# Two attention layers in one trunk: the value products move behind the next block's scores, and the second layer's V is made of nine products instead of twelve

## The chip, the cores and the metric

The kernel runs on one core of a Trainium2 chip, as one launch. The metric is the device time of a run in microseconds (us), as the median of three runs. Engines are named as the profile names them: PE (TensorE matmul; PEld is its weight load), DVE (VectorE), ACT (ScalarE), POOL (GpSimd), SP (the queue that issues most DMAs).

## The reference

The input is x, 16 sequences of 128 tokens with 128 features, and a context of the same shape. Four layers follow one another, each added to x:

```python
x = x + L0_xattn(ctx, layernorm(x), ctx)     # 16 heads of 64, causal mask, softmax over 128 keys
x = x + L0_ffn(layernorm(x))                 # FP4-quantised gate/up/down, 352 hidden
x = x + L1_xattn(layernorm(x), ctx)          # 16 heads of 64, two softmaxes:
#   keys 0..76  ("text"):  k = ctx @ Wk,    v = ctx @ Wv
#   keys 77..127 ("image"): k = ctx @ Wk_ip, v = ctx @ Wv_ip
#   out = (softmax_text @ v_text + softmax_image @ v_image) @ Wo + bo
x = x + L1_ffn(layernorm(x))                 # router, top 2 of 8 experts, 512 hidden
```

What matters for the change is the second attention layer's V: 77 keys of a sequence are multiplied by Wv and the other 51 by Wv_ip. The order of the keys is free, as long as the probabilities of a key meet the V row of the same key.

## The kernel before

The 16 sequences form 8 groups of two (PAIR); the 16 heads form 4 blocks of four (BLOCKS, HB). Both attention layers run in one trunk of 128 steps, n = 0 to 127: layer 0 is n 0 to 63, layer 1 is n 64 to 127. A group takes 8 steps, a block two: an even step and the odd step behind it, called a pair here. Each engine has its own function `step`, called for each n in turn (trunk, L366), so the order of the work on an engine is written out by hand, and each engine runs its list strictly in that order, held only by semaphores.

PE (step, L792), even step: the scores of the block, 16 matmuls (L815, each with 64 rows of the array); Q and K of the next block, three passes each (L404 to L406: low times high, high times low, high times high); the transposes of the probabilities of step n-2 (L853, 4 matmuls); the values, probabilities times V, of the block two pairs back (L868, 16 matmuls, each with 64 columns of the array). Odd step: V of the block (project_v, L646), the transposes (L853), the output projection with Wo (L885, 8 matmuls). V takes 6 matmuls in layer 0. In layer 1 the staged context is held twice, once with the text keys and zeros elsewhere (st_hi[0], st_lo[0]) and once with the image keys and zeros elsewhere ([1]), and V is the sum over both: 2 sequences x 2 weights x 3 passes = 12 matmuls.

ACT (L1037), even step: it copies Q and K from PSUM (L909, L916 or L924), the transposed probabilities (L1034) and the heads (L1027), and takes the exponential of the scores (L1068 in layer 0, L1072 in layer 1). Two switches (heads_first, probs_first) set the order of these copies. Odd step: it copies V (L1061), takes the exponential, then does the FFN's work of the step, then copies the transposed probabilities.

DVE (L1384): in an even step first the sums (L1361) of the odd step before, the update of x (L1111), the mask and maxima (L1333, L1339) or the maxima and the subtraction (L1351, L1377) of both steps of the pair, and the inverse of the sums (L1369). In layer 0 most sums of odd steps come from ACT's own accumulator instead. In an odd step: the sums and inverse of the even step.

POOL (L1614) scales the exponentials to probabilities (L1625, in layer 1 one instruction for the text keys and one for the image keys) and stages the context of the next group at the end of a group (stage, L1590).

The first FFN is woven in from n = 16 (ffn_at): its eight slots s0 to s7 fall on steps 0, 2, 3, 4, 5, 7, 8, 9 of each ten. Slot s0 has the back half of one quantisation on DVE, s1 its end, s2 the transposes and copies of the hidden layer (L658, L970), s3 the down product (L676) and the quantisation of x, s4 the gate product, a tanh on ACT (L979) and its product on DVE (L1307), s5 a transpose, s6 the up product, s7 a quantisation. The norm of x after layer 1 is woven in by D_AT: the four steps of each group of sequences at which its slots 4 to 7 run. In the last of them PE transposes into the bank of the probabilities (turn_d, L704), ACT copies the high part (L940) and DVE the low part (L1209). The transposes of the next step wait for that low part. From n = 114 the router of the experts is woven in (routes).

## Time and profile before

| | us |
|---|---|
| median of 3 runs (lowest, highest) | 666.07 (665.52, 667.85) |
| profiled execution, own time | 668.6 |
| its span | 666.9 |
| PE busy / PEld busy | 612.9 / 560.3 |
| DVE busy / ACT busy / POOL busy | 492.2 / 464.8 / 308.2 |
| mean granted TensorE clock | 0.969 |

A matmul's busy time is modelled and overlaps the next one's: a matmul of 0.28 us can be followed by another 0.12 us later. So the pace of PE is read from the distance between starts, and a "busy" PE can still hold short gaps. In the timeline a pair begins at the first matmul of L815.

### The profile page before, as it was taken

To read this page: it belongs to the slowest core of one execution; us is meant where nothing else is said; L and a number is where in the kernel's file an instruction comes from. 1 tells how busy PE (TensorE), PEld (TensorE's weight loads), DVE (VectorE), ACT (ScalarE), POOL (GpSimd) and SP (SyncE) were. 2 spreads that over 40 slices of the span, in tenths; PEclk is the share of its full clock that TensorE was granted. 3 is DMA by queue.
4 is the path that set the end of the run, shared out by engine and by line. 5 is a ranking of instruction groups with operands and counts; after the bars stand their busy time and mean duration, and the time that the engine had idled before them with its cause. 6 is when DMAs were issued, how large, how long until landed. Compare 5 with 4: busy or idle time off the path is not lost.

```text
span 666.9 us, 16387 instructions
## 1 busy us (share of the span) xinstructions
PE 612.9 (92%) x5665; PEld 560.3 (84%) x5665; DVE 492.2 (74%) x1255; ACT 464.8 (70%) x1347; POOL 308.2 (46%) x444
## 2 busy tenths in 40 slices
PE   5898999999999999999999999999999879989990
PEld 5787888988889899999989988888888868979990
DVE  6588787798887978888797986876655665656654
ACT  5987889988888896666666766667555354646762
POOL 4365344444444434354445343445265574456450
PEclk9998999999999999999999999999889798989995
DMA  9800000000000000336664020000000032112215
GB/s 221 260 2 1 1 1 1 2 2 2 1 2 2 2 17 2 128 79 125 124 123 93 25 57 1 1 2 2 1 21 25 21 103 57 49 57 65 70 51 198
DMA packets 49626, 33.33 MB, mean 50 GB/s; under 512 B 9524, under 2 KB 46104, under 8 KB 49544
## 3 DMA queue, kind: packets, MB, share of 16 engines
q1 hardware_dynamic: 47272, 27.61, 17.3%
q0 software_dynamic: 2272, 4.67, 2.1%
q8 instruction: 46, 0.75, 0.5%
q14 instruction: 36, 0.29, 0.2%
HBM read 17.64 MB, written 14.63 MB: 48 GB/s over the span
## 4 chain that ended last, share of the span: by engine, by line
PE 53%; issue 14%; DVE 11%; POOL 9%; ACT 8%; DMA 2%; SPq 0%; POOLq 0%; DVEq 0%; another core or an unknown queue 0%; ACTq 0%
PE ps_j L646 6%; PE ps_h L868 6%; PE ps_s L815 6%; PE ps_h L885 5%; PE ps_t L853 5%; PE ps_j L404 4%; ACT scores L1068 4%; PE ph L1811 4%; PE py L1822 3%; POOL probs L1625 3%; POOL xs_scratch L1736 3%; PE ps_j L405 3%; PE ps_j L406 3%; PE pf L676 2%; DVE sums L1361 1%
## 5 line engine op out<-in xcount | busy, mean ns | idle before, releaser
L1625 POOL TENSOR_TENSOR probs<-scores,rsums 128x308 f32<-128x308 f32 (+1 forms) x192 | 152.2, 807 | 202.4 <-DVE rsums L1369 202.1
L1068 ACT ACTIVATE scores<-scores,neg_max 128x128 f32<-128x128 f32 x256 | 91.7, 398 | 0.0
L1034 ACT ACTIVATE probsT<-ps_t 128x512 f32<-128x512 f32 x128 | 76.4, 597 | 18.5 <-PE ps_t L853 18.2
L853 PE MATMUL ps_t<-ident,probs 128*128 128x128 f32 x512 | 79.4, 278 | 5.5 <-POOL probs L1625 4.4
L1361 DVE TENSOR_REDUCE sums<-scores 128x4 f32<-128x308 f32 (+2 forms) x156 | 66.3, 459 | 23.2 <-ACT scores L1072 11.7
L909 ACT ACTIVATE QT<-ps_j 128x512 f32<-128x512 f32 x64 | 38.3, 598 | 51.9 <-PE ps_j L406 51.9
L868 PE MATMUL ps_h<-probsT,V 128*64 128x128 f32 x1024 | 71.1, 281 | 2.3 <-DVE x_sb L1111 2.3
L885 PE MATMUL ps_h<-Wo,headsT 128*128 128x128 f32 x512 | 69.8, 280 | 2.0 <-ACT headsT L1027 1.9
L853 PEld LDWEIGHTS ps_t<-ident,probs 128*128 128x128 f32 x512 | 60.4, 143 | 9.4 <-POOL probs L1625 7.3
L885 PEld LDWEIGHTS ps_h<-Wo,headsT 128*128 128x128 f32 x512 | 63.8, 196 | 3.4 <-ACT headsT L1027 3.4
L868 PEld LDWEIGHTS ps_h<-probsT,V 128*64 128x64 f32 x1024 | 55.6, 138 | 13.2 <-issue 11.7
L646 PE MATMUL ps_j<-l_hi,st_lo 128*128 128x256 f32 x192 | 61.2, 319 | 0.9 <-ACT QT L909 0.9
L815 PE MATMUL ps_s<-KT,QT 64*128 64x128 f32 x800 | 59.0, 288 | 0.8 <-ACT KT L916 0.8
L1872 ACT ACTIVATE hT<-ph,w1s 128x128 f32<-128x128 f32 x156 | 45.5, 371 | 16.4 <-PE ph L1811 13.9
L1891 POOL DMA_INDIRECT y_scratch<-ysb,xt x39 | 38.6, 991 | 37.6 <-DVE ysb L1948 35.0
L646 PE MATMUL ps_j<-l_hi,st_hi 128*128 128x256 f32 x192 | 55.6, 290 | 0.0
L646 PE MATMUL ps_j<-l_lo,st_hi 128*128 128x256 f32 x192 | 55.6, 289 | 0.0
L815 PEld LDWEIGHTS ps_s<-KT,QT 64*128 64x128 f32 x800 | 49.4, 190 | 7.0 <-issue 1.9
L1351 DVE TENSOR_REDUCE neg_max<-ps_s 128x8 f32<-128x616 f32 x64 | 42.4, 663 | 16.5 <-PE ps_s L815 16.5
L1061 ACT ACTIVATE V<-ps_j 128x512 f32<-128x512 f32 x64 | 37.8, 590 | 23.0 <-PE ps_j L646 22.9
L1027 ACT ACTIVATE headsT<-ps_h 128x512 f32<-128x512 f32 x64 | 38.3, 598 | 20.1 <-PE ps_h L868 20.0
L1811 PE MATMUL ph<-xT,w1s 128*128 128x128 f32 x312 | 44.3, 284 | 5.0 <-ACT hT L1872 3.2
(248 smaller groups left out, 1640.2 us busy)
## 6 DMA issues: line engine op xcount, KB each, us to landing
xs_scratch<-xs SPq DMA_DIRECT2D x8, 1032.0 KB, 8.3
xt<-xs_scratch SPq DMA_DIRECT2D x39, 64.5 KB
w1b<-in_L_ffn_w_dram SPq DMA_DIRECT2D x1, 2048.0 KB, 10.4
big_raw<-in_L_ffn_w_dram SPq DMA_DIRECT2D x8, 256.0 KB
ysum<-y_scratch SPq DMA_DIRECT2D x4, 512.0 KB, 5.3
Wo<-in_L_xattn_Wo_dram SPq DMA_DIRECT2D x2, 512.0 KB, 5.2
out_dram<-x_sb SPq DMA_DIRECT2D x4, 256.0 KB, 2.4
x_sb<-in_x_dram SPq DMA_DIRECT2D x3, 256.0 KB, 9.2
```

Source lines behind the costliest of these rows:

```text
L646: ins = nc.tensor.matmul(dst, st[i][:, bb, :], w[:, cols], start=(n == 0), stop=(n == 3 * len(SEGS[lay]) - 1))
L815: ins = nc.tensor.matmul(ps_scores[half][:, j * S:(j + 1) * S], QT[hb % 2][rows, t, bb, :], k_home(m)[rows, t, bb, :], start=True, stop=True)
L853: ins = nc.tensor.transpose(ps_pT[:, j * S:(j + 1) * S], probs[s % 2][:, j, :], ident[:, :])
L868: ins = nc.tensor.matmul(ps_heads[par * HD:(par + 1) * HD, (bb * TILES + t) * S:(bb * TILES + t + 1) * S], V[hr % 2][:, bb, i * HD:(i + 1) ...
L885: ins = nc.tensor.matmul(ps_heads[:, bb * D:(bb + 1) * D], headsT[:, bb, t, :], Wo[lr][:, hr * TILES + t, :], start=(t == 0), stop=(t == T ...
L1034: nc.scalar.activation(probsT[(s - 2) % 4][:, :, :].rearrange("p h s -> p (h s)"), ps_pT[:, :], ACT.Copy).then_inc(SS["pT_copied"], 1)
L1068: ins = nc.scalar.activation(scores[s % 4][:, j, :], scores[s % 4][:, j, :], ACT.Exp, bias=neg_max[:, 0, s % 4, j:j + 1], **total)
L1351: nc.vector.tensor_reduce(pair_of(neg_max[:, i, :, :], s).rearrange("p t h -> p (t h)"), pair_bank()[:, :, k0:k1], AX_X, ALU.max, negate=T ...
L1361: ins = nc.vector.tensor_reduce(sums[:, p4, i, :], scores[p4][:, :, k0:k1], AX_X, ALU.add)
L1625: ins = nc.gpsimd.tensor_tensor(probs[(s - 1) % 2][:, :, k0:k1], scores[r][:, :, k0:k1], rsums[:, r, i, :].rearrange("p (h a) -> p h a", a ...
L1811: ins = nc.tensor.matmul(ph[k // 2][:, (k % 2) * P:(k % 2 + 1) * P], w1s[i % 3][:, 0, k * P:(k + 1) * P], xT[i % 2][:, :], start=True, sto ...
L1872: nc.scalar.activation(hT[i % 2][:, k, :], ph[k // 2][:, (k % 2) * P:(k % 2 + 1) * P], ACT.Silu, bias=w1s[i % 3][:, 0, HID + k:HID + k + 1 ...
```

## The change

Two things are changed. (1) On PE the values go to the front of the even step, directly behind the scores, and the output projection goes to the end of the same even step; before, the values ended the even step and the output ended the odd one. ACT copies the heads first in an even step; it copies the transposed probabilities before it takes the exponential, in odd steps before it copies V too. DVE updates x in the odd step, behind both steps' maxima. The router's middle part goes ahead in odd steps, and D_AT is changed so that the last slot of a norm falls on an even step. (2) In layer 1 the staged context gets a new layout of 128 key columns: one copy holds text keys only, 64 of sequence 1 and 64 of sequence 0 (st[0], column 0); one holds the 13 text keys left over of each (st[1], column 0); one holds the 51 image keys of both (st[0], column 1). The first makes one half of the bank in three passes with Wv, the other two make the other half in three passes with Wv and three with Wv_ip: 9 matmuls. The keys of a sequence so stand in a rotated order, and the upper 64 rows of the two halves are swapped. V is copied by three ACT instructions (64 partitions x 512, and twice 64 x 256), POOL writes the probabilities with three instructions, and the staging of a group takes 12 casts for 4.

```diff
+        HALF, IP = S // 2, S - TEXT
+        MIXED = TEXT - HALF
...
-        D_AT = [(81, 83, 84, 85), (91, 93, 94, 95), (101, 103, 104, 105), (106, 107, 108, 109), (111, 112, 113, 114),
-                (116, 117, 118, 119), (124, 125, 126, 127), (NG * STEPS + 4,)]
+        D_AT = [(81, 83, 84, 86), (91, 93, 94, 96), (101, 103, 104, 106), (107, 108, 109, 110), (111, 112, 113, 114),
+                (115, 116, 117, 118), (123, 124, 125, 126), (NG * STEPS + 4,)]
...
@@ PE, project_v
-                for bb in range(PAIR):
-                    dst = bank[:, bb * 256:(bb + 1) * 256]
+                if lay == 0:
+                    parts = [[(0, 0, WV[0][0])], [(0, 1, WV[0][0])]]
+                else:
+                    parts = [[(1, 0, WV[1][0]), (0, 1, WV[1][1])], [(0, 0, WV[1][0])]]
+                for half, terms in enumerate(parts):
+                    dst = bank[:, half * 256:(half + 1) * 256]
                     n = 0
-                    for i, (w_hi, w_lo) in enumerate(WV[lay]):
+                    for i, c, (w_hi, w_lo) in terms:
                         for st, w in ((st_lo, w_hi), (st_hi, w_lo), (st_hi, w_hi)):
-                            ins = nc.tensor.matmul(dst, st[i][:, bb, :], w[:, cols], start=(n == 0),
-                                                   stop=(n == 3 * len(SEGS[lay]) - 1))
+                            ins = nc.tensor.matmul(dst, st[i][:, c, :], w[:, cols], start=(n == 0),
+                                                   stop=(n == 3 * len(terms) - 1))
                             n += 1
@@ PE, step (values, turn_probs and output hold the code that stood inline)
+                if s % 2 == 0:
+                    values(n, s, G, first)
+                else:
+                    for u, t in routes(n):
+                        route_mid(u, t)
                 if f["s"] in (1, 4):
                     slot(**f)
...
                 if f["s"] in (0, 3, 5, 6, 7):
                     slot(**f)
-                for u, t in routes(n):
-                    route_mid(u, t)
...
+                if s % 2 == 0:
+                    for u, t in routes(n):
+                        route_mid(u, t)
+                turn_probs(n, s, first)
                 if f["s"] == 2:
                     slot(**f)
+                if s % 2 == 0:
+                    output(s, G, prev, lay, first)
                 if fd["s"] == 7:
@@ ACT, step
-                heads_first = lay == 0 and HEADS_FROM <= n
-                probs_first = s % 2 == 0 and n < ROUTE_FROM[0]
+                if s % 2 == 0:
+                    copy_heads(s, G, first)
+                else:
+                    for u, t in routes(n):
+                        route_mid(u, t)
...
-                    if probs_first:
-                        copy_probs(n, s, G, first)
-                    if heads_first and par == 0:
-                        copy_heads(s, G, first)
+                    copy_probs(n, s, G, first)
                     if par == 1:
                         act.wait_ge(SS["v_ready"], m + 1)
...
+                            nc.scalar.activation(V[hb % 2][0:HALF, :, :].rearrange("p b d -> p (b d)"),
+                                                 v_bank(m)[0:HALF, :], ACT.Copy)
+                            for b in range(PAIR):
+                                ins = nc.scalar.activation(V[hb % 2][HALF:P, b, :],
+                                                           v_bank(m)[HALF:P, (1 - b) * 256:(2 - b) * 256], ACT.Copy)
...
@@ DVE, step: the update of x leaves the head of the even step
+                if s % 2 == 1 and (s >= 5 or not first) and s < STEPS + 4:
+                    if s >= 5:
+                        update_x(G * BLOCKS + (s - 5) // 2, g)
+                    else:
+                        update_x(G * BLOCKS + (s - 5) // 2, GROUPS - 1 if prev != lay else g - 1)
                 part(0)
@@ POOL
+                        for i, c, k0, k1, at, b in ((0, 0, 0, HALF, 0, 1), (0, 0, MIXED, TEXT, HALF, 0),
+                                                    (1, 0, 0, MIXED, IP, 0), (1, 0, HALF, TEXT, HALF, 1),
+                                                    (0, 1, TEXT, S, 0, 0), (0, 1, TEXT, S, TEXT, 1)):
+                            ins = nc.gpsimd.tensor_copy(st[i][:, c, at:at + k1 - k0], src[:, g, k0:k1, b])
...
+            def scale_rotated(dst, src, inverse):
+                by_b = src[:, :, :].rearrange("p (t b) k -> p t b k", b=PAIR)
+                inv = inverse.rearrange("p i (t b a) -> p i t b a", b=PAIR, a=1)
+                text = dst[:, :, :].rearrange("p (t b) k -> p t (b k)", b=PAIR)[:, :, IP:IP + PAIR * TEXT]
+                nc.gpsimd.tensor_tensor(text.rearrange("p t (b k) -> p t b k", b=PAIR), by_b[:, :, :, 0:TEXT],
+                                        inv[:, 0, :, :, :].broadcast_to([P, TILES, PAIR, TEXT]), ALU.mult)
+                for b, at in ((0, 0), (1, TEXT)):
+                    ins = nc.gpsimd.tensor_tensor(
+                        dst[:, :, :].rearrange("p (t b) k -> p t b k", b=PAIR)[:, :, b, at:at + IP],
+                        by_b[:, :, b, TEXT:S], inv[:, 1, :, b, :].broadcast_to([P, TILES, IP]), ALU.mult)
+                return ins
```

## Rows read from the trace of the kernel before

**Rows 1.** Windows: length, then PE, PEld, DVE, ACT, POOL busy (count), granted clock, DMA
```profile
11.02:70.70 59.68, 54.15 (x500) 48.38 (x500) 42.86 (x104) 48.35 (x156) 30.58 (x31) 0.97 0.35 99
70.70:249.17 178.47, 172.91 (x1710) 156.00 (x1709) 148.33 (x331) 156.92 (x504) 77.54 (x88) 1.00 0.01 3
249.17:458.92 209.75, 207.19 (x1991) 189.12 (x1990) 175.54 (x422) 138.93 (x354) 95.88 (x185) 1.00 0.29 60
458.92:536.48 77.56, 72.95 (x600) 66.47 (x599) 46.81 (x160) 41.87 (x85) 36.80 (x56) 0.91 0.05 17
316.67:357.63 40.96, 40.44 (x391) 36.85 (x390) 36.14 (x90) 27.55 (x70) 19.62 (x40) 1.00 0.71 127
165.00:203.18 38.18, 36.96 (x365) 33.52 (x364) 32.84 (x73) 32.78 (x108) 16.72 (x20) 1.00 0.01 2
```

**Rows 2.** The same view, a stretch inside the pairs n = 82 to 86
```profile
331.10:348.86 17.76, 17.24 (x166) 15.49 (x164) 17.55 (x43) 11.43 (x27) 7.96 (x14) 1.00 0.66 120
```

**Rows 3.** Timeline of PE, the pair at n = 80: start, us, instruction
```profile
316.67 1.16 PE L815 MATMUL ps_s<-KT,QT 64*128 64x128 f32 x16
...
319.90 0.60 PE L853 MATMUL ps_t<-ident,probs 128*128 128x128 f32 x4
320.44 1.09 PE L868 MATMUL ps_h<-probsT,V 128*64 128x128 f32 x16
...
322.53 0.28 PE L646 MATMUL ps_j<-l_hi,st_lo 128*128 128x256 f32 x1
...
323.94 0.60 PE L853 MATMUL ps_t<-ident,probs 128*128 128x128 f32 x4
324.38 1.06 PE L885 MATMUL ps_h<-Wo,headsT 128*128 128x128 f32 x8
325.37 1.16 PE L815 MATMUL ps_s<-big_raw,QT 64*128 64x128 f32 x16
```

**Rows 4.** Timeline of DVE in the same pair
```profile
317.90 0.80 DVE L1351 TENSOR_REDUCE neg_max<-ps_s 128x8 f32<-128x616 f32 x1 [0.70 <-PE ps_s L815]
...
319.17 1.28 DVE L1377 TENSOR_TENSOR scores<-ps_s,neg_max 128x616 f32<-128x616 f32 x2
...
326.00 0.95 DVE L1307 SCALAR_TENSOR_TENSOR silu_h<-silu_h,pf 128x352 f32<-128x352 f32 x2 [2.17 <-ACT silu_h L979]
```

**Rows 5.** Timeline of ACT in the same pair
```profile
324.14 0.60 ACT L1061 ACTIVATE V<-ps_j 128x512 f32<-128x512 f32 x1 [0.48 <-PE ps_j L646]
...
325.16 0.81 ACT L979 ACTIVATE silu_h<-pf 128x352 f32<-128x352 f32 x2
```

**Rows 6.** Timeline of PE around and in the pair at n = 86
```profile
341.56 0.41 PE L704 MATMUL ps_t<-ident,xs 128*128 128x128 f32 x2 [0.45 <-ACT probsT L1034]
341.90 1.16 PE L815 MATMUL ps_s<-big_raw,QT 64*128 64x128 f32 x16
...
347.11 0.60 PE L853 MATMUL ps_t<-ident,probs 128*128 128x128 f32 x4
```

**Rows 7.** Timeline of DVE in the pair at n = 86
```profile
345.02 1.28 DVE L1377 TENSOR_TENSOR scores<-ps_s,neg_max 128x616 f32<-128x616 f32 x2
...
348.13 0.42 DVE L1275 TENSOR_TENSOR fqT_lo<-pf,fqT_hi 128x256 fp32r<-128x256 f32 x1
```

**Rows 8.** Timeline of PE, odd step of the pair at n = 48
```profile
192.77 0.87 PE L658 MATMUL pf<-ident,silu_h 128*128 128x128 f32 x6 [0.51 <-DVE silu_h L1165]
```

**Rows 9.** Groups with shapes kept apart, 250 to 460 us: busy us, mean ns
```profile
L1625 POOL TENSOR_TENSOR probs<-scores,rsums 128x308 f32<-128x308 f32 x49 | 39.0, 795 | 65.3 <-DVE rsums L1369 65.2
L1625 POOL TENSOR_TENSOR probs<-scores,rsums 128x204 f32<-128x204 f32 x49 | 27.0, 551 | 0.0
L1596 POOL CAST st_lo<-ctxT_lo 128x102 fp32r<-128x102 f32 x7 | 1.9, 275 | 0.0
L924 ACT ACTIVATE KT<-ps_j 128x256 f32<-128x256 f32 x28 | 10.7, 384 | 5.2 <-PE ps_j L406 4.7
```

**Rows 10.** Timeline of PE at n = 116
```profile
476.69 1.95 PE L733 MATMUL pf<-rw_sb,hidT 128*128 128x8 f32 x16 [0.90 <-DVE hidT L1463]
```

More of the change, by code:

```diff
@@ L790, in route_end, with turn_probs @@
                         ranks(u, False)
+            def turn_probs(n, s, first):
+                if (s >= 2 or not first) and s - 2 < STEPS:
+                    pe.wait_ge(SS["probs_ready"], n - 1)
+                    wait_pos(pe, SS["pT_copied"], n - 2)
+                    if d_at(n - 1)["s"] == 7:
+                        pe.wait_ge(SS["loD"], d_at(n - 1)["d"] + 1)
+                    if n - 1 == BIAS_AT:
+                        pe.wait_ge(MS["bias_copied"], 1)
+                    for j in range(HB):
+                        ins = nc.tensor.transpose(ps_pT[:, j * S:(j + 1) * S], probs[s % 2][:, j, :], ident[:, :])
+                    ins.then_inc(SS["pT_ready"], 1)
@@ new lines, in output @@
+            def output(s, G, prev, lay, first):
+                if (s >= 4 or not first) and s < STEPS + 4:
+                    mr = G * BLOCKS + (s - 4) // 2
+                    hr = ((s - 4) // 2) % BLOCKS
+                    lr = prev if s < 4 else lay
+                    pe.wait_ge(SS["heads_copied"], mr + 1)
+                    if first and s == 4:
+                        pe.wait_ge(s_wo0, 16)
+                    if isinstance(G, int) and G == GROUPS and s == 4:
+                        pe.wait_ge(s_small, 16 * 6)
+                    for bb in range(PAIR):
+                        for t in range(TILES):
+                            ins = nc.tensor.matmul(ps_heads[:, bb * D:(bb + 1) * D], headsT[:, bb, t, :],
+                                                   Wo[lr][:, hr * TILES + t, :],
+                                                   start=(t == 0), stop=(t == TILES - 1))
+                    ins.then_inc(SS["out_ready"], 1)
```

102 lines of the change are left out of this document (39 added, 63 removed).

## The prediction, made before the changed kernel ran

> **What bounds the kernel now.** I read the windows by stage first. In the trunk PE is busy 172.9 of 178.5 us in layer 0 behind the start, and 207.2 of 209.8 us in layer 1 up to n = 113 [rows 1]. The reader is to see that nothing else is near that. But DVE is not far: 175.5 of 209.8 us, and in the ten steps from n = 80 it has 36.1 us of work in 40.96. In the ten steps from n = 41 in layer 0 DVE has 32.8 and ACT 32.8 of 38.18 us [rows 1]. So PE sets the pace, and two engines at 86 to 88% stand behind it with their lists in a fixed order. From n = 114 (458.92 to 536.48) PE is busy 72.95 of 77.56 us at a mean granted clock of 0.91, DVE only 46.8: there the router's chain from engine to engine takes part [rows 1].
>
> Second, the timeline of PE in one pair [rows 3]. The starts follow each other without holes: 815, Q, the FFN's down product, 853, 868, gate, V, 853, 885, and the next 815 at 8.70 us. Shorter work on PE is therefore worth its full length here, if the others follow. Third, the timelines of DVE and ACT in that pair show where they do not: DVE sits idle 2.17 us before the gate's product L1307, for a tanh of ACT, although PE never waits [rows 4, 5].
>
> **What the change takes off PE.** V in layer 1: 12 products start at 322.53 and the next group at 323.94, so 1.41 / 12 = 0.118 us each [rows 3]. Three go in each of 32 blocks: 96 x 0.118 = 11.3 us.
>
> The change of array shape: four transposes take 0.54 us of starts when the values follow (319.90 to 320.44), and 0.44 when the output follows (323.94 to 324.38) [rows 3]. Each entry into or exit from the work with half rows or half columns so costs 0.10 us. A pair has four such borders: into and out of the scores, into and out of the values. With values directly behind scores it has three, if going from half rows to half columns costs one border: 0.10 x 63 = 6.3 us. The trace has no such neighbours, so this one border is bounded by 0 and 0.20 us; I take 0.10, the border that every row shows. The Trainium skill ("TensorEngine Tiling (Array Packing)", Key Properties) says that changing the tiling mode drains the engine; by it the border stays and the sum is as here, while without it another 6.3 us would go.
>
> Together 17.6 us if PE were the only limit: 668.6 (the profiled execution's own time) would become 651.0.
>
> **What it costs elsewhere.** The price of one instruction less on PE is small work on others. V's copy in ACT, 0.60 us [rows 5], becomes that and two more of 256 columns at 0.384 [rows 9]. Successive ACT starts are some 0.1 us closer than the durations, so V takes 1.05 us for 0.5, +0.55 per block. POOL scales 308 and 204 elements in 795 and 551 ns [rows 9], 2.35 ns an element and 0.07 fixed; the image part in two instructions of 102 costs 0.31 each, +0.07 us a step, bounds 0 and 0.55 (two as dear as the whole). The staging has 12 casts for 4; at 0.2 to 0.275 us each [rows 9] +1.3 to 2.2 us a group. POOL is busy 95.9 of 209.8 us [rows 1]; both hide there, as PE needs the staged context a whole pair later and the probabilities of a step two steps later.
>
> The real cost is order. Before, ACT takes V and the odd step's exponential as soon as V is there: V at 324.14, tanh begun at 325.16, before the next pair's scores start at 325.37 [rows 3, 5]. After, the copy of the transposed probabilities stands in front of both, and it waits for the odd step's transposes, which now are PE's last work of the pair. Let S be the start of the next scores; the transposes end at S - 0.1. Then ACT: copy 0.5, V 1.05 (0.5 in layer 0), exponential 0.6 (four, 1.6, in layer 0): the odd exponential is done at S + 2.1 in layer 1 and about S + 2.6 in layer 0. Queued behind it on DVE is everything, because in layer 1 the sums of that exponential are the first thing in DVE's even step. Sums 0.66: maxima from S + 2.8. In the pair at n = 80 they started at S + 1.23 (317.90 - 316.67) and the subtraction ended at S + 3.8 [rows 3, 4]; it will end at S + 5.3. When FFN slot s4 lies in the odd step, the tanh is behind too: copy 0.5, V 1.05, exponential 0.5, tanh 0.8, and in front of them a sum of squares that DVE releases late. DVE's gate product ends at S + 3.8 to 4.3; before, 326.95 - 325.37 = S + 1.6 [rows 3, 4] (326.95 is its start and its 0.95 us). Its idle before L1307 grows from 2.17 to about 2.9 us.
>
> The cover for this is on PE's side: the values (0.93 us) and the border now lie before the even transposes, so these may come 1.0 us later; the odd ones too (output 0.89 us for values). Against 1.5 to 2.5 us of delay on DVE this is not enough where DVE has no slack. In ten steps PE's floor is 40.96 - 5 x 0.45 = 38.7 us; DVE's work is 36.1, its wait for the tanh 2.9, and in about one light pair it is early and waits another 1.3 for the odd exponential: 40.3. So nearly all of the 2.25 us per ten steps is given back, by waits of PE for slot s2's copies (0.45, at the down product) and for late probabilities.
>
> One more: the last slot of a norm now is on an even step. Before, PE waited 0.45 us there for a copy of ACT that came last in its step (before L704, 341.56) [rows 6]; four such waits, with the gap around each 0.6, go: -2.4 us. But the transposes right behind V now need DVE's low part, and DVE does that at the end of its even step. At n = 86, 96 and 106 FFN slot s0 is in the same step. From the end of the subtraction (346.30) to the end of s0 (348.55) is 2.25 us [rows 7]. With the subtraction ending at S + 5.3, the low part is ready at S + 5.3 + 2.25 + 0.4 = S + 8.0. PE would be there at S + 5.2 (347.11 - 341.90 [rows 6]) + 0.89 output + 0.25 turn - 0.45 = S + 5.9. That is a stall of 2.1 us, three times 6.3. At n = 86 DVE is 2 us later still, since from 331.10 to 348.86 it has 17.6 us of work in 17.8 [rows 2] and can recover nothing (s6 and s7 come before): +2.0, counted with the late even transposes below. At 110, 114, 118 and 126 longer PE work covers it.
>
> **The sum, by stage.**
> - Start, 11.02 to 70.70: PE is busy 54.15 of 59.68 us at a clock of 0.97 [rows 1]; the output of the first blocks no longer follows right behind its copy. Borders 7 x 0.1, and 1.3 of the 5.5 idle us: -2.0.
> - Layer 0, 70.70 to 249.17: 24 pairs x 0.10 = -2.4. In the full FFN cycles DVE gets its gate product later (S + 4.4) and the quantised hidden layer, for which PE already waits 0.51 us at n = 49 [rows 8], comes about 0.6 later in each of s0, s2 and s3's pairs, +1.9 for ten steps, 2.3 times: +4.4. Together +2.0.
> - Layer 1, 249.17 to 458.92: 25 pairs x 0.45 = -11.3; waits before L704 -2.4; back come 5 x 0.45 (down), 3.3 (late even transposes behind s6 and s7), 6.3 (low part): -1.8.
> - Routing, 458.92 to the end of the trunk: products 7 x 0.35, borders 0.7; back 1.6, as DVE's router products, for which PE waits 0.90 us at n = 116 [rows 10], stand behind the later subtraction: -1.6.
>
> Sum -3.4 us, so 668.6 becomes 665.2. The profiled execution lies 2.5 us above the median of the three runs shown, 666.07; the forecast for a median is 666.07 - 3.4 = 662.7 us. Its own range is 659 to 667.
>
> **The rivals.**
> *PE keeps the pace.* DVE swallows the delay in its 4.8 idle us per ten steps, since most of them lie in pairs where the wait would fall. For it: PE had no wait for DVE longer than 0.5 us in these rows [rows 6, 8], and the even transposes gain 1.0 us of cover. Against it: 36.1 + 2.9 already is more than the new floor of 38.7. Then 17.6 less some 4 us for the low part, 13.6, or a few us less: 650 to 657 beside the median, say 653.
> *The late exponential decides.* The place is ACT's odd step, copy before V and exponential; the price is 1.5 us of DVE per pair in layer 1 and, where FFN work fills both steps, a PE stall of 1 to 2 us in three pairs of every ten steps instead of one. It decides as soon as DVE ends a pair more than about 3 us behind the next scores (subtraction + exponential + copy would then pass the next values). For 4.6 FFN cycles in layer 0 and 5 in layer 1, 1.5 us more each than in my sum: +14 on top of -3.4, that is 676 at worst, 671 in the middle. For it: DVE without a hole over two and a half pairs [rows 2]. Against it: layer 0's first pairs have no FFN work.
> *Nothing comes of it.* Gain and waits cancel in every stage, as the pace passes from PE to DVE: 666 within 0.3%.
>
> **How the numbers follow.** 0.3% (2 us) is what a measurement of this kernel can tell from none. My forecast has 0.42 (0.32 of it faster, 0.10 within the bound), PE keeping the pace 0.20, the late exponential 0.28, nothing 0.10. So faster 0.52, same 0.20, slower 0.28. The range takes most of the outer two and the unknown border (6.3 us below): 650 to 674.
>
> **What would show it.** In the profile after: V as 9 products in 1.05 us; the same 0.10 border once between L815's and L868's successors; DVE idle before the sums of odd steps in layer 1, released by ACT's exponential, where before there was none; idle before the gate product near 2.9 us; no wait before the turn of L704, but PE idle of about 2 us before the transposes at n = 87, 97 and 107, released by DVE's low part; a pair without FFN in layer 0 at 6.3 us for 6.41. The prediction is wrong if ten steps in layer 1 from n = 80 take under 39.5 or over 42 us, or if the routing stage moves by more than 4 us either way.

## The result, and the profile after

The changed kernel takes 675.07 us (median of 4 runs, 673.28 to 675.75), the kernel before beside it 665.80 (4 runs, 664.50 to 667.85): ratio 1.0123, 95% interval 1.0092 to 1.0154. It is slower by 9.3 us. The forecast was 662.7, and the time lies outside the range of 650 to 674. The profiled execution took 675.75 us for 668.6 before, so the traces show 7.2 of the 9.3 us.

The windows by stage of the changed kernel, cut at the same steps as [rows 1]: start; layer 0; n = 64 to 113; routing; the last row is the ten steps from n = 80.

```profile
11.00:67.22 56.22, 51.38 (x500) 46.58 (x501) 43.26 (x101) 47.44 (x156) 30.23 (x31) 1.00 0.36 104
67.22:246.30 179.08, 169.27 (x1710) 154.49 (x1710) 150.16 (x331) 155.94 (x502) 77.75 (x88) 1.00 0.01 3
246.30:465.92 219.62, 199.88 (x1915) 180.74 (x1914) 175.66 (x418) 156.74 (x396) 108.22 (x288) 0.99 0.28 58
465.92:543.19 77.27, 70.70 (x581) 63.80 (x580) 48.74 (x165) 47.35 (x101) 40.37 (x78) 0.91 0.05 16
313.68:360.76 47.08, 40.54 (x376) 36.47 (x375) 38.42 (x90) 31.64 (x81) 23.94 (x70) 0.96 0.66 121
```

Beside [rows 1] the start is 3.5 us shorter, layer 0 0.6 longer, routing 0.3 shorter, and n = 64 to 113 is 9.9 us longer (219.62 for 209.75), although PE's busy time fell by 7.3 us there. ACT's rose by 17.8 and POOL's by 12.3; DVE's stayed. The ten steps from n = 80 take 47.08 us for 40.96, over the 42 that the prediction named as its sign of being wrong. Something makes PE wait. The timeline of PE shows where (n = 80 to 82, then n = 86):

```profile
316.49 0.28 PE L407 MATMUL ps_j<-xnT_hi,l_hi 128*128 128x256 f32 x1
317.22 1.60 PE L681 MATMUL pf<-dnT,hqT 128*128 128x128 f32 x12 [0.46 <-ACT hqT L989]
...
321.24 0.28 PE L651 MATMUL ps_j<-l_hi,st_lo 128*128 128x256 f32 x1
...
322.30 0.60 PE L806 MATMUL ps_t<-ident,probs 128*128 128x128 f32 x4
...
325.18 1.09 PE L820 MATMUL ps_h<-probsT,V 128*64 128x128 f32 x16 [1.19 <-ACT probsT L1051]
...
329.38 0.41 PE L405 MATMUL ps_j<-ctxT_hi,l_lo 128*128 128x308 f32 x1 [1.45 <-ACT QT L926]
...
346.41 1.11 PE L806 MATMUL ps_t<-ident,probs 128*128 128x128 f32 x4 [2.02 <-POOL probs L1651]
347.31 1.92 PE L838 MATMUL ps_h<-Wo,headsT 128*128 128x128 f32 x8
```

V does take 1.06 us now (321.24 to 322.30), as forecast. But the values wait for a copy of ACT, K's second half for another, and the even transposes for POOL. What ACT does in that stretch, from its odd step n = 81 on:

```profile
323.95 0.31 ACT L951 ACTIVATE fsq<-fy 128x128 f32<-128x128 f32 x1 [3.53 <-DVE fy L1223]
...
324.55 0.58 ACT L1051 ACTIVATE probsT<-ps_t 128x512 f32<-128x512 f32 x1
325.03 0.58 ACT L1082 ACTIVATE V<-ps_j 64x512 f32<-64x512 f32 x1
325.62 0.65 ACT L1085 ACTIVATE V<-ps_j 64x256 f32<-64x256 f32 x2
326.30 0.64 ACT L1097 ACTIVATE scores<-scores 128x512 f32<-128x512 f32 x1
326.95 0.82 ACT L996 ACTIVATE silu_h<-pf 128x352 f32<-128x352 f32 x2
...
328.72 0.60 ACT L926 ACTIVATE QT<-ps_j 128x512 f32<-128x512 f32 x1
```

V occupies ACT from 325.03 to 326.30, 1.27 us. The odd exponential starts 3.47 us behind the next scores (322.83), the tanh 4.12, and Q's copy at 328.72, though Q's products ended at 327. DVE meanwhile:

```profile
316.19 0.74 DVE L1385 TENSOR_REDUCE sums<-scores 128x4 f32<-128x308 f32 x2 [1.82 <-ACT scores L1097]
...
319.97 1.87 DVE L1159 TENSOR_SCALAR q_scale<-q_scale 128x16 f32<-128x16 f32 x1
...
323.49 0.42 DVE L1223 SCALAR_TENSOR_TENSOR fy<-fmean,x_sb 128x256 f32<-128x256 f32 x1
...
327.81 0.95 DVE L1331 SCALAR_TENSOR_TENSOR silu_h<-silu_h,pf 128x352 f32<-128x352 f32 x2 [2.99 <-ACT silu_h L996]
```

And the waits summed over n = 64 to 113 (who waits, for whom: us in total, times, longest), first DVE's and one of ACT's, then PE's:

```profile
DVE sums L1385 <- ACT scores L1097: 19.6, 15, 2.2
DVE silu_h L1331 <- ACT silu_h L996: 10.9, 4, 3.6
ACT fsq L951 <- DVE fy L1223: 9.9, 5, 3.5
...
PE ps_t L806 <- POOL probs L1651: 4.1, 5, 2.0
PE ps_j L405 <- ACT QT L926: 4.1, 5, 1.4
PE ps_t L806 <- DVE xnT_lo L1233: 3.8, 3, 1.8
```

The first three in the same view of the kernel before:

```profile
DVE sums L1361 <- ACT scores L1072: 8.9, 12, 1.7
DVE silu_h L1307 <- ACT silu_h L979: 8.0, 4, 3.3
ACT fsq L934 <- DVE fy L1199: 2.4, 3, 0.8
```

So there is a circle: ACT waits for DVE (3.53 us, for the norm's fy, in front of the copy of the probabilities), DVE then for ACT (2.99 us), and PE for both. If the distances between starts on PE that are longer than usual for their two lines are added up, PE's pauses grew from 11.3 to 30.4 us.

The delay shows in every pair of the stage. Let S be the start of the next scores, as in the prediction. The odd exponential ended at S - 0.1 in most pairs before; it ends at S + 2.5 in 21 of 25 now. DVE's subtraction ended 4.3 us behind the scores of its own pair on average before, and ends 6.4 behind them now.

The shapes apart, the same stretch, busy us and mean ns of one:

```profile
L1085 ACT ACTIVATE V<-ps_j 64x256 f32<-64x256 f32 x48 | 15.6, 373 | 0.3
L1082 ACT ACTIVATE V<-ps_j 64x512 f32<-64x512 f32 x24 | 13.9, 578 | 0.0
L1079 ACT ACTIVATE V<-ps_j 128x512 f32<-128x512 f32 x1 | 0.6, 591 | 0.0
...
L1648 POOL TENSOR_TENSOR probs<-scores,rsums 128x308 f32<-128x308 f32 x48 | 37.9, 791 | 63.7 <-DVE rsums L1393 63.6
L1651 POOL TENSOR_TENSOR probs<-scores,rsums 128x102 f32<-128x102 f32 x96 | 34.1, 376 | 0.0
```

A copy of 64 partitions takes about as long as one of 128 (578 and 591 ns). So the three cost 578 + 2 x 373 = 1324 ns for 591.

### The profile page after: what moved, and what is told of

Same layout as the page of the kernel before. It is cut to its first block, busy times and chain, and to the rows that moved or that the text cites. A ratio compares the mean times of both kernels' runs of the same rounds, so it can differ in the third digit from the quotient of the medians.

```text
span 673.1 us, 16398 instructions
## 1 busy us (share of the span) xinstructions
PE 596.3 (89%) x5569; PEld 544.7 (81%) x5569; DVE 496.1 (74%) x1255; ACT 487.9 (72%) x1411; POOL 324.6 (48%) x574
## 4 chain that ended last, share of the span: by engine, by line
PE 36%; DVE 26%; ACT 19%; issue 12%; POOL 3%; DMA 3%; another core or an unknown queue 1%; SPq 0%; DVEq 0%; ACTq 0%; POOLq 0%
PE ph L1856 5%; PE py L1867 4%; ACT scores L1093 4%; PE ps_t L806 3%; PE ps_h L838 3%; DVE scores L1357 3%; PE ps_j L651 3%; DVE neg_max L1363 2%; DVE sums L1385 2%; PE ps_j L405 2%; PE ps_s L866 2%; PE ps_h L820 2%; ACT V L1085 2%; ACT probsT L1051 2%; DVE neg_max L1375 2%
## 5 line engine op out<-in xcount | busy, mean ns | idle before, releaser
L1667 POOL TENSOR_TENSOR probs<-scores,rsums 128x512 f32<-128x512 f32 x64 | 70.6, 1104 | 99.6 <-DVE rsums L1393 99.4
L1648 POOL TENSOR_TENSOR probs<-scores,rsums 128x308 f32<-128x308 f32 x64 | 49.2, 769 | 94.3 <-DVE rsums L1393 94.2
L820 PE MATMUL ps_h<-probsT,V 128*64 128x128 f32 x1024 | 71.0, 281 | 10.4 <-ACT probsT L1051 5.2
L651 PE MATMUL ps_j<-l_hi,st_lo 128*128 128x256 f32 x160 | 50.0, 312 | 1.1 <-ACT QT L926 1.0
L1097 ACT ACTIVATE scores<-scores 128x512 f32<-128x512 f32 x64 | 40.4, 631 | 10.9 <-DVE scores L1401 8.6
L1357 DVE TENSOR_TENSOR scores<-ps_s,causal 128x512 f32<-128x512 f32 x64 | 43.0, 674 | 4.6 <-PE ps_s L866 4.4
L405 PE MATMUL ps_j<-ctxT_hi,l_lo 128*128 128x256 f32 (+4 forms) x136 | 40.0, 294 | 7.2 <-ACT QT L926 6.8
L1856 PEld LDWEIGHTS ph<-xT,w1s 128*128 128x128 f32 x312 | 39.9, 199 | 8.0 <-issue 6.9
```

The costliest lines, as they stand in the source:

```text
L405: nc.tensor.matmul(psum, lo[:, w_cols], act_hi, start=start, stop=False)
L651: ins = nc.tensor.matmul(dst, st[i][:, c, :], w[:, cols], start=(n == 0), stop=(n == 3 * len(terms) - 1))
L820: ins = nc.tensor.matmul(ps_heads[par * HD:(par + 1) * HD, (bb * TILES + t) * S:(bb * TILES + t + 1) * S], V[hr % 2][:, bb, i * HD:(i + 1) ...
L1357: nc.vector.tensor_tensor(scores[s % 4][:, :, :], bank_of(s % 2), causal[:, :].rearrange("p (a s) -> p a s", a=1).broadcast_to([P, HB, S]) ...
L1667: ins = nc.gpsimd.tensor_tensor(probs[(s - 1) % 2][:, :, :], scores[r][:, :, :], rsums[:, r, 0, :].rearrange("p (h a) -> p h a", a=1) .bro ...
L1856: ins = nc.tensor.matmul(ph[k // 2][:, (k % 2) * P:(k % 2 + 1) * P], w1s[i % 3][:, 0, k * P:(k + 1) * P], xT[i % 2][:, :], start=True, sto ...
```

## The experiments

Each was timed beside the kernel before. "Stage" is n = 64 to 113 of its one profiled execution, by the starts of the scores. The absolute times differ between chips (the kernel before: 659.42 to 666.02 in the six sets), so only the ratios are compared. The profiled execution of one_copy, 662.9 us, is its slowest, so its stage is if anything shorter; those of old_turn and v_swap lie 4 us above their medians too, that of exp_old_turn 5 us below. Four versions serve only to tell causes apart and do not compute the reference: one_copy, one_copy_exp and nine_one_copy leave out the exchange of V's halves, pool_before the rotation of the keys. Order of ACT's odd step in layer 1: P copy of the probabilities, V copy of V, E exponential. The old order is V, E, and P at the end of the step. The theories: A, the odd exponential behind two copies of ACT; B, the rotated keys; C, the norm's slot and K's second half; then D, V's two extra copies, and E, POOL's extra work.

| kernel | orders | V products, copies | E/V/P | norm's last slot | ratio (95%) | stage |
|---|---|---|---|---|---|---|
| before | old | 12, 1 | VE..P | odd | 1 | 209.7 |
| changed | new | 9, 3 | PVE | even | 1.0123 (1.0092, 1.0154) | 219.6 |
| order_only | new | 12, 1 | PVE | even | 1.0046 (1.0019, 1.0073) | 212.6 |
| nine_only | old | 9, 3 | VE..P | odd | 1.0171 (1.0138, 1.0204) | 213.0 |
| exp_first | new | 9, 3 | EPV, both layers | even | 1.0291 (1.0262, 1.0320) | 212.4 |
| old_turn | new | 9, 3 | PVE | odd | 1.0060 (1.0037, 1.0084) | 215.4 |
| one_copy | new | 9, 1 | PVE | even | 0.9947 (0.9916, 0.9979) | 210.8 |
| pool_before | new | 9, 3 | PVE | even | 1.0106 (1.0071, 1.0141) | 218.4 |
| exp_first_l1 | new | 9, 3 | EPV | even | 0.9985 (0.9961, 1.0008) | 212.1 |
| v_last_l1 | new | 9, 3 | PEV | even | 1.0021 (0.9994, 1.0048) | 212.6 |
| exp_old_turn | new | 9, 3 | EPV | odd | 0.9993 (0.9968, 1.0017) | 210.2 |
| exp_twelve | new | 12, 1 | EPV | even | 0.9973 (0.9946, 1.0001) | 209.2 |
| nine_late_v | old | 9, 3 | EV..P | odd | 1.0089 (1.0065, 1.0113) | 209.8 |
| before_late_v | old | 12, 1 | EV..P | odd | 0.9986 (0.9961, 1.0010) | 207.7 |
| nine_one_copy | old | 9, 1 | VE..P | odd | 0.9946 (0.9928, 0.9965) | 207.7 |
| one_copy_exp | new | 9, 1 | EPV | even | 0.9932 (0.9900, 0.9964) | 207.9 |
| v_swap | new | 9, 1 + POOL | PVE | even | 1.0084 (1.0055, 1.0112) | 219.0 |
| v_swap_exp | new | 9, 1 + POOL | EPV | even | 1.0026 (0.9998, 1.0053) | 217.5 |
| two_copies | new | 9, 2 | EPV | odd | 0.9988 (0.9957, 1.0018) | 210.0 |
| exp_twelve_ot | new | 12, 1 | EPV | odd | 0.9920 (0.9891, 0.9949) | 205.7 |

### Each part alone

order_only is the changed kernel with the second part of the change taken back (project_v, V's copy, the staging, POOL's scaling as on the minus side of the diff); nine_only is the kernel before with that part alone.

> The new orders on all engines, but V in layer 1 in twelve products, one ACT copy, two POOL scalings a step and four casts a group, as before. Theory A (the order of ACT decides: in odd steps the copy of the probabilities and V stand before the exponential, and nothing queued behind it on DVE can start): the damage stays. Layer 0 as in the changed kernel (179.1 us for n = 16 to 63). In layer 1 n = 64 to 113 PE gets 8.8 us of products back, of which part fills the 30 us of stalls; ACT loses 0.55 us a block from its chain. Stage 218 to 222 us, total 673 to 677. Theory B (the rotated keys cost: two more ACT copies, a third POOL instruction and 12 casts make the stalls): the stage n = 64 to 113 falls below 213 us in spite of the three more products, total 666 or less.

> The old orders, with the nine products, the rotated keys, three V copies, three POOL scalings and 12 casts. Theory A (the order decides): part two alone is a gain or near it: 25 blocks x 0.35 us = 8.8 us less on PE in n = 64 to 113, of which 0.55 us a block on ACT gives something back, so the stage is 203 to 209 us for 209.7, and the total 658 to 665. Theory B (the rotated keys cost): the stage is longer than 212 us, the total over 668.

Theory A missed in both runs (stages of 212.6 us for its 218 to 222, and 213.0 for its 203 to 209); theory B, that the rotated keys cost, met its numbers in both. Two thirds of the loss belong to the nine products: without them the new orders cost 0.5%, and they alone cost 1.7% (both together 1.2%, with intervals that overlap). So the order is not the only cause, and the question is what the nine products bring with them.

Not all of it lies in the stage, which is 3.3 us longer in nine_only. Its routing (n = 114 to 126) takes 81.43 us for 77.56 before [rows 1], at a lower granted clock, and that of pool_before, a run below, 71.03 us at a higher one:

```profile
460.04:541.47 81.43, 73.79 (x581) 66.99 (x580) 46.13 (x157) 47.98 (x99) 39.98 (x77) 0.87 0.05 15
464.33:535.36 71.03, 66.24 (x582) 59.75 (x581) 47.28 (x161) 47.54 (x101) 37.48 (x58) 0.98 0.05 17
```

Each is a single execution, and no run tells how much of such a difference the kernel makes and how much the execution. In the stage the clock is 0.98 to 1.00 in every version. So causes are read from the stage, and what they are worth in all from the medians.

### What the nine products bring

one_copy leaves out the exchange of the halves:

```diff
-                            nc.scalar.activation(V[hb % 2][0:HALF, :, :]..., v_bank(m)[0:HALF, :], ACT.Copy)
-                            for b in range(PAIR):
-                                ins = nc.scalar.activation(V[hb % 2][HALF:P, b, :],
-                                                           v_bank(m)[HALF:P, (1 - b) * 256:(2 - b) * 256], ACT.Copy)
+                        nc.scalar.activation(V[hb % 2][:, :, :]..., v_bank(m)[:, :], ACT.Copy)
```

> The changed kernel, but ACT copies V in layer 1 with one instruction of 128 x 512 (about 0.60 us) in place of three (0.58 + 0.37 + 0.37 = 1.33 us): the exchange of the upper halves is left out. The first runs showed that nine products cost in either order of the work (the old order alone with nine products is 12 us slower than before). Theory D (the cost is the 0.73 us more of ACT in each block, in front of the odd exponential and so of all of DVE): most of the difference between nine and twelve products goes and the 8.8 us of products are gained too: n = 64 to 113 takes 208 to 213 us for 219.6, the ratio to before 0.995 to 1.004. Rival E (POOL's third scaling and its twelve casts): the stage stays within 3 us of 219.6, ratio 1.009 to 1.014.

pool_before gives POOL its old two scalings a step and four casts a group, in the old order of the keys; the nine products and the three copies stay.

> The changed kernel, but POOL scales the probabilities with two instructions a step and stages the context with four casts, in the old order of the keys (the rotation of the keys is left out); the nine products and the three V copies stay. Theory D (V copies on ACT): the stage n = 64 to 113 stays within 3 us of 219.6, ratio 1.009 to 1.013. Rival E (POOL): PE's waits for the probabilities (4.1 us in 5 places) and DVE's slow small operations beside the three-part scaling go; the stage falls to 214 us or less, ratio 1.005 or less.

Their windows of n = 64 to 113, first one_copy:

```profile
248.11:458.89 210.78, 198.69 (x1916) 181.37 (x1915) 178.00 (x418) 139.16 (x348) 108.27 (x288) 0.98 0.26 60
```

pool_before:

```profile
245.96:464.33 218.37, 200.45 (x1915) 181.88 (x1914) 173.50 (x418) 156.80 (x396) 93.22 (x182) 0.98 0.25 58
```

That decides it. 17.6 us less of ACT (139.16 for 156.74) are worth 8.8 us in the stage and 1.8% in all; 15 us less of POOL are worth 1.3 us and 0.2%, which the measurement can't tell from nothing. In one_copy the odd exponential ends at S + 1.7 in most pairs, for S + 2.5, and DVE's subtraction 5.6 us behind the scores, for 6.4. The two extra copies of V are the price; POOL's extra work costs nothing that these runs can tell.

### The place of the copies

exp_first takes the exponential, then the probabilities, then V in ACT's odd steps of both layers; exp_first_l1 does so in layer 1 alone; v_last_l1 moves only V. In short, with "V" and "exponential" for their instructions:

```diff
-                    copy_probs(n, s, G, first); V; exponential
+                    exponential; copy_probs(n, s, G, first); V        # exp_first, exp_first_l1
+                    copy_probs(n, s, G, first); exponential; V        # v_last_l1
```

> The changed kernel, but in odd steps ACT takes the exponential first, then copies the transposed probabilities, then V. Theory A (late odd exponential): DVE's idle before the sums of odd steps (19.6 us in 15 places in layer 1) goes to under 10 us; PE's stalls in n = 64 to 113 fall from 30 to 20 us or less, the stage from 219.6 to 210 us or less, total 663 to 668. What could hinder: the values two steps later wait for the probabilities' copy, V's bank comes free 0.6 us later. Theory C (the stalls come from the turn on the even step and from K's second half behind the Q copy): the stage stays within 2 us of 219.6, total 673 to 676.

In layer 1 it brought most of what was expected (212.4 us for 219.6, where 210 or less was expected), and DVE's wait before the sums fell from 19.6 to 1.2 us. In layer 0 it lost 10.4 us, and the start 5.6: there the exponential is four instructions (1.6 us), and the copy that the values need stood behind them. PE's waits of exp_first in layer 0 (1.1 us in the changed kernel):

```profile
PE ps_h L820 <- ACT probsT L1051: 21.5, 22, 1.7
```

> The changed kernel with ACT's odd step in layer 1 as exponential, copy of the probabilities, V; layer 0 as changed. With this order in both layers n = 64 to 113 took 212.4 us for 219.6, while layer 0 and the start lost 16 us. Theory A for layer 1 (the odd exponential behind two copies holds DVE): the stage is 211 to 214 us, all before as in the changed kernel, the ratio 1.000 to 1.004. Rival: the gain in layer 1 was only the longer pairs of layer 0 handing over a DVE with more slack; then the stage stays over 217 us and the ratio over 1.008.

> The changed kernel with ACT's odd step in layer 1 as copy of the probabilities, exponential, V: only V's 1.33 us leave the front of the exponential, the wait for PE's transposes stays in front of it. Theory D (V's copies are the price): as good as with the exponential first, stage 211 to 214 us, ratio 1.000 to 1.004. If the wait for the transposes is the price instead: 216 to 219 us, ratio 1.006 to 1.011. K's first product may wait for V's copy up to 0.5 us a pair, which would show on PE before the first K product.

Both stages are as expected (212.1 and 212.6 us; the ratio 0.9985 lies just under its range): in layer 1 the late odd exponential is what holds DVE, and V in front of it is most of what makes it late. The waits of DVE for the exponential in the stage, 19.6 us in the changed kernel, first in exp_first_l1, then in v_last_l1:

```profile
DVE sums L1395 <- ACT scores L1098: 1.2, 4, 0.5
```

```profile
DVE sums L1395 <- ACT scores L1098: 7.9, 12, 1.7
```

V in front of the exponential was 11.7 of the 19.6 us; the copy of the probabilities, with its wait for PE's transposes, was the other 6.7. In time the first is worth 1.0%, and the second can't be told from nothing (1.0021 against 0.9985, with intervals that overlap).

nine_late_v and before_late_v move V behind the exponential in the old order, in layer 1, again in short:

```diff
-                    V; exponential; ...; copy_probs(n, s, G, first)
+                    exponential; V; ...; copy_probs(n, s, G, first)
```

> The old orders and nine products, but ACT takes V behind the exponential in the odd steps of layer 1. With V in front this was 1.0171. Theory D (the three V copies in front of the exponential are the price): most of it goes, 0.990 to 1.000. Rival: in the old order the copies of the probabilities and the heads at the end of ACT's steps stand behind V in either case, and PE's waits for them (headsT 3.1 us, the turn 5.7 us) stay: 1.008 or more.

This lies in the rival's range: half of the loss went (1.0171 to 1.0089) and not most of it. PE's pauses before the output (2.9 us) and before the turn (4.5 us) stayed, as the rival had it. Probably V's copies there hold up the copies of the probabilities and heads at the end of ACT's step; no run moves those.

> The kernel before with only this exchange (exponential before V in the odd steps of layer 1). DVE waited 8.9 us in 12 places for the odd exponential there, and PE had stalls of 11 us in n = 64 to 113, none of them for DVE. So within 0.3% of before, 0.997 to 1.003; if it gains over 0.5%, DVE already set the pace of these pairs before the change.

As expected, no difference in time that can be told, though its stage is 2.0 us shorter: with one copy of V in the old order, the order of V and the exponential hardly matters.

one_copy_exp is exp_first_l1 and nine_one_copy is nine_only, each with the single copy of one_copy.

> Exponential first in layer 1, and V in one copy with the exchange of the halves left out. It is the bound for the run before. One cause: 0.995 to 1.000, as each of the two alone (0.9947 and 0.9985). Two causes that add: 0.985 to 0.992, and DVE's idle in n = 64 to 113 falls under 25 us.

> Old orders, nine products, V in one copy with the exchange of the halves left out; POOL's three scalings and twelve casts stay. With three copies this was 1.0171, with the three behind the exponential 1.0089. If the copies by their length are all of it, the 11.3 us of products show at last: 0.984 to 0.992. If DVE and ACT pace these pairs anyway, products of PE are worth little: 0.995 to 1.001.

one_copy_exp lies between its two ranges (0.9932), far nearer to one cause: effects that add would give 0.981, and DVE's idle is 30 us, not under 25. A short copy is worth 1.8% where it stands in front of the exponential (1.0123 to 0.9947) and 0.5% behind it (0.9985 to 0.9932). nine_one_copy shows what nine products are worth if their copies were free: 0.54%, 3.6 us of the 11.3 that come off PE, as PE's pauses in n = 64 to 113 are 17.6 us there for 11.3 before. So free copies would not bring back most of the 11.3 either.

### The norm's last slot

old_turn is the changed kernel, exp_old_turn is exp_first_l1, with the whole of D_AT as before:

```diff
-        D_AT = [(81, 83, 84, 86), (91, 93, 94, 96), (101, 103, 104, 106), (107, 108, 109, 110), ...
+        D_AT = [(81, 83, 84, 85), (91, 93, 94, 95), (101, 103, 104, 105), (106, 107, 108, 109), ...
```

> The changed kernel with the old steps of the norm, so the last slot is on an odd step again. Theory C (the turn costs): the waits for DVE's low part (4.6 us before the transposes at n = 87, 97, 107, in part also the late even transposes) go, and the waits before the turn that the change removed (2.4 us) do not come back in full: 670 to 672.5. Theory A: the waits only move, since DVE and ACT are late anyway: 674 to 677.

> The changed kernel with the exponential first in ACT's odd steps of layer 1, and the norm's last slot back on the odd steps. Apart they measured 0.9985 and 1.006, for 1.0123 of the changed kernel. If the two effects add (different waits of PE: the late even transposes and the low part): 0.992, about 5 us below before. Rival: once the exponential is on time, the norm's place no longer matters, or the turn on the odd step finds PE waiting again (2.5 us before the turn): 0.996 to 0.999.

The old steps gained 0.6% where the exponential was late (1.0123 to 1.0060, as theory C had it) and nothing that can be told where it was early (0.9985 to 0.9993; a sum of effects would be 0.992): the effects do not add. In the stages the old steps gained 4.2 and 1.9 us.

### Versions that compute all of the reference

exp_twelve is exp_first_l1 with the second part of the change taken back.

> The same order (exponential first in the odd steps of layer 1), but V in twelve products with one copy, two scalings and four casts: the reorder alone. If the nine products are worth their 8.8 us on PE plus 2.5 in the routing once V's copies stand behind the exponential, this is slower than the version with nine (0.9985): 1.008 to 1.014. If DVE bounds these pairs, so that products of PE are worth nothing: within 0.3% of 0.9985.

Within 0.3% of the version with nine, as the second case had it: with the exponential in time, the 11.3 us of products and the price of the copies cancel. Nine products with a single copy (one_copy_exp, 0.9932) are 0.4% faster than this, so the products are worth some 3 us here and the copies cost as much.

v_swap and v_swap_exp have the single copy of one_copy up to n = 113, and on POOL, behind the scaling of the odd step (the semaphores between the copies are left out here):

```diff
+                    pool.wait_ge(SS["v_copied"], m + 1)
...
+                    nc.gpsimd.tensor_copy(V_spare[HALF:P, :], v[HALF:P, 0, :])...
...
+                    nc.gpsimd.tensor_copy(v[HALF:P, 0, :], v[HALF:P, 1, :])...
...
+                    nc.gpsimd.tensor_copy(v[HALF:P, 1, :], V_spare[HALF:P, :])...
```

> The changed kernel, but up to n = 113 ACT copies V with one instruction and POOL exchanges the upper halves in SBUF afterwards (three copies of 64 x 256, each waiting for the one before), two pairs before PE needs them. Unlike the run with one copy and no exchange (0.9947) it computes all of the reference. If POOL's time is free: 0.994 to 0.998. If the exchange on POOL (some 2 us a pair) delays the scaling of the probabilities or slows DVE beside it: 1.002 to 1.010.

> The same, with the exponential first in ACT's odd steps of layer 1. One cause (the copies matter only in front of the exponential): no better than 0.9985, within 0.3% of it. Two causes: 0.990 to 0.994. With a price on POOL: over 1.000.

The exchange on POOL costs about as much as on ACT (1.0084 for 1.0123, and 1.0026 for 0.9985, both within the intervals). Its three copies in v_swap (mean ns of one), and what PE waited for there:

```profile
L1685 POOL COPY V<-V_spare 64x256 f32<-64x256 f32 x23 | 9.2, 399 | 1.4
L1683 POOL COPY V<-V 64x256 f32<-64x256 f32 x23 | 9.2, 399 | 1.4
L1681 POOL COPY V_spare<-V 64x256 f32<-64x256 f32 x23 | 9.1, 395 | 4.8 <-ACT V L1082 2.0 <-POOL probs L1654 0.2
...
PE ps_j L653 <- POOL st_lo L1629: 7.6, 3, 3.0
PE ps_t L808 <- POOL probs L1654: 6.3, 8, 1.5
```

The staging of the next context stands behind the exchange in POOL's list, and V's products wait for it: a wait that the kernel before did not have.

two_copies is exp_old_turn with one instruction for the upper halves:

```diff
-                            for b in range(PAIR):
-                                ... V[hb % 2][HALF:P, b, :], v_bank(m)[HALF:P, (1 - b) * 256:(2 - b) * 256]
+                            ... V[hb % 2][HALF:P, :, :], v_bank(m)[HALF:P, :].rearrange(...)[:, ::-1, :]
```

> Nine products, exponential first in the odd steps of layer 1, the norm's last slot on the odd steps, and V's upper halves exchanged by one ACT instruction that reads them in reversed order: two copies of 64 x 512 (2 x 0.58 = 1.16 us) for three (1.33). It computes all of the reference. With three copies this was 0.9993. 0.17 us of ACT in 25 blocks is 4.2 us of ACT work; with one copy (0.73 us less) the ratio fell by 0.005, so in proportion by 0.001: 0.996 to 1.000. If the reversed reading is slow (over 0.8 us) it is over 1.001.

```profile
L1083 ACT ACTIVATE V<-ps_j 64x512 f32<-64x512 f32 x24 | 14.2, 592 | 0.3
```

The reversed reading costs nothing extra (592 ns for 578), but the version is no better than with three.

exp_twelve_ot is exp_old_turn with the second part of the change taken back.

> The same orders with twelve products, one copy, two scalings and four casts. With the norm's slot on the even step it was 0.9973, and moving it to the odd one gained 0.6% where the exponential was late and nothing where it was early. The waits for DVE's low part (4.2 us in 4 places) go, the wait before the turn comes back (2.5 us): 0.993 to 0.998. If it is under 0.995, this is the fastest version that computes all.

This is the fastest version that computes all: 0.9920 (0.9891 to 0.9949), 660.55 us for 666.02, a little below the range expected. Its interval touches that of exp_twelve (0.9946 to 1.0001), but the stage is 3.5 us shorter. It is part one of the change (values behind the scores), with the exponential first in layer 1 and the norm's slots where they were, and V as before. Its window of n = 64 to 113:

```profile
246.02:451.72 205.70, 202.08 (x1991) 187.22 (x1990) 176.13 (x422) 141.08 (x353) 94.96 (x184) 1.00 0.29 62
```

PE is busy 202.08 of 205.70 us, with more products than two_copies in a shorter stage.

## Why the prediction was wrong

- **The step that failed** is "The real cost is order", and with it what "back come" in the sum of layer 1 (249.17 to 458.92). That sum gave -1.8 us; the stage came out at +9.9. The order with twelve products costs 0.5% (order_only); most of the loss is V's two extra copies in front of the odd exponential (one_copy, 1.8%). The sum priced them at +0.55 us a block (1.05 for 0.5); by starts they take 1.27, +0.77, and so the odd exponential ends at S + 2.5 and not at S + 2.1. In the old orders, where nothing of part one can be the reason, they cost 2.3% (1.0171 against 0.9946), 5.3 us of it in the stage.
- **What the sum named and what it left out.** The named terms were about right: PE's pauses before the turn [rows 6] went; the low part cost 4.6 us before three odd transposes (forecast 6.3), the even transposes 3.8 (3.3), the down product 1.9 (2.25). It left out 12.7 us of pauses in other places: K's second half behind Q's copy 5.6 us in 8 pairs, the values 2.5 (behind the probabilities' copy, once behind DVE's update of x), output behind the heads 1.7, the hidden layer's transposes 1.7, the gate 1.2. I followed the delay through DVE and not down ACT's own list, in which Q's copy stands behind all of it. Nor did it carry from pair to pair: the subtraction was to end at S + 5.3; at n = 80 it ends at S + 5.7, at n = 82 at S + 9.0, since ACT stood 3.53 us in front of its copy for DVE's fy.
- **The rival was half right, and its number was luck.** "The late exponential decides" had the place (ACT's odd step) and the point (DVE ends a pair over 3 us behind the scores), and exp_first_l1 bears it out in layer 1. But it put the cause in the order and half of its 14 us in layer 0. Layer 0 lost 0.6 us in all, and layer 1 went 11.7 us past my sum where the rival's 5 cycles of 1.5 us give 7.5. That 676 at worst stands beside 675.07 is two misses that cancel. "DVE without a hole over two and a half pairs" [rows 2] was the row to weigh more.
- **The borders.** I took each entry and each exit as 0.10 us, from rows that show an entry only. By single starts in the pair at n = 28, before, an entry lengthens one distance by some 0.10 us and an exit two: the one from the last product of the group (0.20 for 0.10) and the next (0.22 for 0.12). Going from scores straight to values lengthens one (0.20 us), as I took for the unknown border. So the pair without FFN had six longer distances and has four, and went from 6.41 to 6.21 us for my 6.3. Under FFN work less came: 8.72 to 8.60 us at n = 50.
- **Other terms.** The start gained 3.5 us (forecast 2.0), layer 0 lost 0.6 (lost 2.0), routing gained 0.3 (gained 1.6), which is below what single executions tell. POOL's instruction of 102 elements takes 376 ns for my 310, within my bounds. That DVE's idle before the gate's product is 2.99 us in the pair shown (forecast 2.9) was luck: the product ends at S + 5.9 and not at S + 3.8 to 4.3. I wrote that DVE had no idle before the sums of odd steps before; it had 8.9 us.
- Of the 9.9 us some 1.3 are clock at one place: behind the stall at n = 86 the four transposes take 0.90 us of starts for 0.44 and the eight products of the output 1.71 (347.31 to 349.02) for 0.89.

What stays open in part is why the norm's old steps gain less with nine products and early exponential (0.9985 to 0.9993) than with twelve (0.9973 to 0.9920). The traces show where: in both the pauses before the odd transposes go, but in exp_old_turn PE pauses 5.6 us in front of the values (in exp_first_l1 2.6), for DVE's update of x and ACT's copy of the probabilities, and in exp_twelve_ot 1.1. No run isolates what holds those two.

## What to carry to other kernels

A layout that saves products on the fullest engine is paid where its result is copied: count the copies by instructions and their columns, not by partitions, and follow the delay down the whole list of the engine that copies. In front of what every other engine waits for, 0.77 us a block cost over 11 us in all; behind it 3.5. Where engines stand at 85% in fixed orders, as here, put the exponential ahead of copies that are needed a pair later, and look at each layer apart: the same exchange gained 7 us in one and lost 10 in the other.

## What the runs showed of the hardware

ACT's copy from PSUM takes nearly the same time for 64 and 128 partitions: 578 and 591 ns for 512 elements, 373 ns for 64 x 256 and 384 for 128 x 256 [rows 9].

A border between matmuls on the whole array and on half rows or half columns costs PE some 0.10 us on entry and 0.20 on exit, and from half rows straight to half columns 0.10, by the starts at n = 28 in the two traces.

The tiny DVE operation L1159 (128 x 16) took 1.87 us at 319.97, for a median of 0.18 over its 19 executions (of several sizes). It ends at 321.84, when POOL's work of that stretch does:

```profile
319.78 0.70 POOL L1648 TENSOR_TENSOR probs<-scores,rsums 128x308 f32<-128x308 f32 x1
320.44 0.68 POOL L1651 TENSOR_TENSOR probs<-scores,rsums 128x102 f32<-128x102 f32 x2
321.07 0.73 POOL L1729 TENSOR_TENSOR x_sb<-x_sb,bo_bc 128x256 f32<-128x256 f32 x1
```

The Trainium skill ("SBUF — State Buffer", "SBUF: two separate sides") says that DVE and GpSimd share a pair of ports as an exclusive lock, where the DVE operation runs in a 2-port mode or has two inputs in SBUF, and that whichever starts first holds it for its whole instruction while the other fully blocks. The row agrees with the block, but shows it longer than one instruction: DVE stood until four POOL instructions on end were over. That it is this lock was not tested by a run, and what POOL's extra instructions cost in all, 0.2% by pool_before, can't be told from nothing.

The granted clock fell behind a stall of PE: after the 2.02 us pause at n = 86 it is 0.65 on average over the next 4.7 us, a mix of both levels, 1.2 and 2.4 GHz, where the same pair before ran at 1.00 from 346.00 to 351.20:

```profile
346.41:351.15 4.74, 4.41 (x24) 4.23 (x24) 4.67 (x11) 1.89 (x4) 2.08 (x6) 0.65 0.35 58
```

So this stall cost more than its own length.
